# One transpose for the row maxima of a group of heads, and a new place for the expert matmuls between the attention steps

## The reference

```python
x = x + LN(attn(LN(x)))      # 16 heads of 16, rotary, causal, window of 250
x = x + LN(ffn(LN(x)))
# ffn: a second attention, 16 heads of 16, rotary, all 512 keys (no mask), rmsnorm, then
shared = swiglu(flat @ W_shared_in) @ W_shared_out
h = swiglu(flat @ W1_shared)
for e in range(8):
    routed = routed + h @ W2_experts[e] * w[:, e:e + 1]   # w: top 2 of 4 in the group chosen
out = rmsnorm(x + shared + routed)
```

## Time and profile before

| | us |
|---|---|
| runs of the kernel before | 2071.21, 2077.92, 2048.68 |
| median | 2071.21 |
| profiled execution, its own time | 2052.56 |
| its span, first to last instruction | 2050.8 |
| TensorE busy (PE) | 1887.0 (92%) |
| VectorE busy (DVE) | 1405.9 (69%) |
| ScalarE busy (ACT) | 829.9 (40%) |
| GpSimd busy (POOL) | 376.7 (18%) |
| granted TensorE clock, mean | 0.954 of full speed |

### The profile page before, as it was taken

The page is one execution under the profiler, slowest core; times in us unless marked ns, Lnnn a source line. Parts: engine busy times, 40 slices in busy tenths (PEclk is TensorE's granted clock), DMA queues, the critical chain, the costliest instruction groups (busy, mean ns, idle before and its releaser), DMA issues.

```text
span 2050.8 us, 28564 instructions
## 1 busy us (share of the span) xinstructions
PE 1887.0 (92%) x9436; PEld 1053.9 (51%) x9436; DVE 1405.9 (69%) x4368; ACT 829.9 (40%) x1730; POOL 376.7 (18%) x669
## 2 busy tenths in 40 slices
PE   6868899999999999999999999999999999999987
PEld 4343363745556364654637455563645546364456
DVE  6447475685778668684876857786676857768367
ACT  3432535335342644335353353426433353533410
POOL 1327014101231012200141012310122101420010
PEclk8565899999999999999999999999999999999999
DMA  3016002201022100311022010221003110130420
GB/s 106 2 62 246 22 22 84 83 2 52 22 94 83 43 11 23 134 43 42 32 89 88 2 52 22 94 83 43 11 23 134 43 43 32 47 119 2 175 82 11
DMA packets 28227, 123.09 MB, mean 60 GB/s; under 512 B 3888, under 2 KB 14768, under 8 KB 23472
## 3 DMA queue, kind: packets, MB, share of 16 engines
q1 hardware_dynamic: 25552, 105.54, 14.1%
q0 software_dynamic: 2528, 15.73, 2.0%
HBM read 101.33 MB, written 18.87 MB: 59 GB/s over the span
## 4 chain that ended last, share of the span: by engine, by line
PE 65%; DVE 26%; issue 6%; ACT 3%; DMA 1%; SPq 0%; POOL 0%; DVEq 0%; ACTq 0%; POOLq 0%
PE ot L780 11%; PE fb L841 10%; PE sm L738 8%; DVE negmax L1194 6%; PE fb L819 5%; PE st L766 5%; PE st L706 3%; PE fb L815 3%; DVE sm L1191 2%; PE st L722 2%; DVE acc L1392 2%; PE fb L837 2%; PE sm L766 2%; PE dn L706 2%; PE dn L792 2%
## 5 line engine op out<-in xcount | busy, mean ns | idle before, releaser
L618 ACT ACTIVATE probs<-st 128x512 f32<-128x512 f32 (+3 forms) x832 | 397.7, 506 | 422.5 <-PE st L766 417.4
L841 PE MATMUL fb<-w_r,h_r 128*128 128x512 f32 x1344 | 388.9, 418 | 0.0
L738 PE MATMUL sm<-k_t,q_t 48*128 48x512 f32 (+3 forms) x864 | 318.7, 449 | 58.3 <-DVE negmax L1191 28.9
L1194 DVE TENSOR_REDUCE negmax<-sm 128x1 f32<-128x512 f32 x416 | 269.4, 685 | 82.1 <-PE sm L738 82.0
L766 PE MATMUL st<-q_t,k_t 64*128 64x512 f32 (+3 forms) x832 | 301.8, 452 | 20.9 <-ACT probs L618 19.9
L738 PEld LDWEIGHTS sm<-k_t,q_t 48*128 48x128 f32 x864 | 144.4, 194 | 316.1 <-DVE negmax L1191 144.8
L841 PEld LDWEIGHTS fb<-w_r,h_r 128*128 128x128 f32 x1344 | 232.7, 189 | 93.2 <-issue 55.8
L1191 DVE CUSTOM_DVE_ANT_0 sm<-sm,mask_qk 128x384 f32<-128x384 f32 (+1 forms) x448 | 203.6, 468 | 112.0 <-PE sm L738 108.4
L780 PE MATMUL ot<-probs,v_s 128*32 128x512 f32 (+3 forms) x2048 | 259.6, 539 | 2.3 <-POOL probs L493 2.3
L452 POOL TENSOR_TENSOR stack<-rot,stack 128x256 fp32r<-128x256 f32 x64 | 50.0, 782 | 1017.4 <-ACT stack L554 1017.4
L766 PEld LDWEIGHTS st<-q_t,k_t 64*128 64x128 f32 x832 | 133.4, 192 | 118.5 <-ACT probs L618 79.2
(11 more groups left out here) (210 smaller groups left out, 2769.1 us busy)
## 6 DMA issues: line engine op xcount, KB each, us to landing
w_r<-w_parts SPq DMA_DIRECT2D x30, 2048.0 KB, 8.0
wup_r<-wup_parts SPq DMA_DIRECT2D x32, 512.0 KB, 4.2
w_parts<-w_r POOLq DMA_DIRECT2D x4, 2048.0 KB, 9.0
x_s<-in_L_attn_query SPq DMA_DIRECT2D x8, 512.0 KB, 4.9
q_t<-rot_b SPq DMA_DIRECT2D x256, 4.0 KB
x_kept<-o_s SPq DMA_DIRECT2D x8, 512.0 KB, 3.1
h_s<-in_L_ffn_W_experts POOLq DMA_DIRECT2D x8, 512.0 KB, 4.9
xa<-x_kept SPq DMA_DIRECT2D x8, 512.0 KB, 3.3
```

What stands on the lines that cost most here:

```text
L618: nc.scalar.activation(probs[:, n % PSLOTS, 0:hi - lo], score_bank(m)[:, 0:hi - lo], ACT.Exp, scale=float(D) ** -0.5).then_inc(s_ex, 1)
L738: mm(max_bank(w, a)[:, 0:hi - lo], q_t[r:r + MROW, b, t * P:(t + 1) * P], k_t[r:r + MROW, b, lo:hi], start=True, stop=True).then_inc(s_sm, 1)
L841: last = mm(fb[q % 2][:, :], h_r[:, h, m, rows], w2_r[:, k % 2, w, m, :], start=(m == 0 and n == 0), stop=(m == NH - 1 and n == 2))
L1194: return v.tensor_reduce(negmax[:, g % 2, n // GH, c:c + 1], max_bank(g * UNITS + n, a)[:, 0:hi - lo], AX.X, ALU.max, negate=True).then_in ...
```

## The change

There are two edits.

First, the four transposes of `max_rows` become one. The split maxima are laid out so that all 32 values of a row (2 halves of the array's rows, 2 parts, 2 heads, 4 tiles) stand side by side, and one transpose of 128x32 puts them into 32 partitions of `dn`, 128 columns wide. ScalarE copies 32x128 in place of 8x512. The four DMAs of a group carry the same bytes, each from 8 partitions of 512 bytes in place of 2 of 2048.

Second, expert pieces move. `QUIET` (first body) becomes 3, 7, 11 and so on to 59, and 61, where it was spread evenly over 6 to 60 (6, 9, 13, 16, 20, 24, 27, 31, 34, 38, 42, 45, 49, 52, 56, 60). `QUIET_OUT` (second body) goes from n = 2, 8, 12 (4, 8, 12 in the first group) to n = 6, 10, 14 (6, 10, 12 in the last). The pieces of the lead end one step earlier in the first body. The split of the hidden rows follows five steps behind its matmul, where it was three.

```diff
-QUIET = spread(4 * NH, 6, 60)
-QUIET_OUT = [g * UNITS + n for g in range(NGR) for n in ((2, 8, 12) if g else (4, 8, 12))]
-HIDDEN_AT = spread(8 * NH - len(QUIET), 4 - LEAD, 3) + QUIET
+QUIET = list(range(3, 60, GH)) + [61]
+QUIET_OUT = [g * UNITS + n for g in range(NGR) for n in (6, 10, 14 if g < NGR - 1 else 12)]
+HIDDEN_AT = spread(8 * NH - len(QUIET), 4 - LEAD, 2) + QUIET
...
-ACT_LAG, DVE_LAG, HIGH_LAG = 1, 2, 3
+ACT_LAG, DVE_LAG, HIGH_LAG = 1, 2, 5
...
-        m_split = sb("m_split", [P, 2, NT, 2, 2, 2], F32R)
-        m_t = rot_b[0:8].rearrange("p h d -> p (h d)")
+        m_split = sb("m_split", [P, 2, 2, 2, 2, NT], F32R)
+
+        M_ROWS = 8 * NT
+        m_t = rot_b[0:M_ROWS].rearrange("p h d -> p (h d)")[:, 0:P]
...
-                            r, m = SK * half + MROW + part, 4 * half + 2 * part
+                            r, m = SK * half + MROW + part, 2 * NT * (2 * half + part)
                             sp.dma_start(q_t[r:r + 1, 2 * g:2 * g + 2, :].bitcast(F32),
-                                         rot_b[m:m + 2].rearrange("p h d -> p (h d)")).then_inc(s_mr[g % 2], 16)
+                                         rot_b[m:m + 2 * NT].rearrange("p h d -> p (h d)")[:, 0:P]
+                                         ).then_inc(s_mr[g % 2], 16)
...
-                copy(m_t, dn[0:8, :]).then_inc(s_mc, 1)
+                copy(m_t, dn[0:M_ROWS, 0:P]).then_inc(s_mc, 1)
...
-                for t in range(NT):
-                    last = nc.tensor.transpose(
-                        dn[0:8, t * P:(t + 1) * P],
-                        m_split[:, g % 2, t].bitcast(F32).rearrange("p h j b -> p (h j b)"), ident[:, :])
+                last = nc.tensor.transpose(dn[0:M_ROWS, 0:P],
+                                           m_split[:, g % 2].bitcast(F32).rearrange("p h j b t -> p (h j b t)"),
+                                           ident[:, :])
                 last.then_inc(s_mp, 1)
...
-                m = negmax[:, g % 2].rearrange("p t (b h) -> p t h b", b=2)
-                hi = m_split[:, g % 2, :, :, 0, :]
-                lo = m_split[:, g % 2, :, :, 1, :]
+                m = negmax[:, g % 2].rearrange("p t (b h) -> p h b t", b=2)
+                hi = m_split[:, g % 2, :, 0]
+                lo = m_split[:, g % 2, :, 1]
```

## The result

| | us |
|---|---|
| runs of the changed kernel | 2124.18, 2167.89, 2115.39, 2127.41 |
| median of all four | 2125.8 |
| ratio to the kernel before | 1.0335, 95% interval 1.0287 to 1.0384 |
| profiled execution, its own time; span | 2124.18; 2122.4 |
| granted TensorE clock, mean (before) | 0.932 (0.954) |

The account below looks back on a forecast made before the run. TensorE was taken to bound both middles, VectorE the second body's lead. 7 x (2.6 - 0.9) = +11.9, entry 0 -3.6 and clock -6.2, together +2.1 on 2052.56, gave 2055 us, range 2018 to 2085.

Parts of the forecast that it names:

- The row of four: Four steps without an expert piece between them take about 2.35 us, two separate pairs 1.32: about 1.0 us lost.
- 2.6 us per entry: Second body: 2.1 us longer in the first group, 1.4 in the second, 0.85 gained in the third, tail 0.
- The tail has four banks, and I see no new wait: 0: Second body's tail: the moved expert pieces were to cost nothing there.
- The first body: First body as a whole: 0.9 us gained per entry, with 0.35 by step 39, 0.33 in the lead, 0.2 in the tail.
- fewer rows of four are new: two in the first group: First body: only steps 7 to 10 and 11 to 14 become new rows of four; step 12 is 1.2 us later.
- at step 19 only 0.3 are left: First body: of the 1.2 us delay at step 12, 0.3 remains at step 19, an expert piece being already done.
- The transposes and the subtraction: One transpose for four saves 0.33 us per call; VectorE's small subtraction no longer waits for GpSimd's, some 1.0 us per first body.
- The merges: Fewer changes between scores and expert work on TensorE: 0 to 0.1 us each, taken as 0, 8 us held for the range.
- the wait moves instead of going: Rival, chance 0.20: GpSimd's subtraction meets another small VectorE instruction near step 23, so that gain and the clock's fail: 2068 us.
- 2 x 3.1 = 6.2 us: Clock term: two falls to half clock in first bodies' middles (entries 6 and 7) go away, saving 6.2 us.
- bunching and the clock: Rival, chance 0.09: second bodies cost 4.5 us plus 3.1 for a clock fall each, first bodies gain nothing: +50, 2102 us.
- TensorE alone counts: Rival, chance 0.15: VectorE's slack swallows all bunching, leaving pure savings of 41 us: 2012 us.

Follow-up runs that it names:

- E1: The single transpose alone on the kernel before, with all expert pieces and lags as before; ratio 1.0057.
- E2: The moves and lags of the change alone on the kernel before, with its four transposes kept; ratio 1.044.
- E5: E1 with the split of the hidden rows five steps behind its matmul in place of three; ratio 0.9907 to the kernel before.
- E9: E5 with one expert piece of the second body moved from step 18 to 20; ratio 0.9993 to the kernel before.
- E7: The changed kernel with the scores of n = 4, 5, 8, 9, 12, 13 in second bodies' middles issued twice; ratio 1.0305 to the kernel before.
- E13: E5 with five maximum scores at the end of the second body's lead issued twice; ratio 0.9881 to the kernel before.
- E8: E1 with first bodies' score matmul of step 18 issued twice and that of step 21 three times; ratio 0.9922 to the kernel before.
- E10: E5 with the second body's expert pieces at n = 7, 11, 15 (7, 11, 12 in the last group); ratio 1.0414 to the kernel before.

## Why the prediction was wrong

**The row of four: right in kind and size.** 2.31 us measured for 2.35, waits of 0.54 for 0.54, a middle 2.1 us longer with one piece fewer. The term "2.6 us per entry" for the second body measured 2.1 + 1.2 = 3.3. What failed there is "The tail has four banks, and I see no new wait: 0": I had not counted that the tail takes over a piece. In it the transposes of the outputs then wait for ScalarE:

```profile
725.81 0.66 PE L795 MATMUL dn<-ident,o_t 128*128 128x128 f32 x4 [0.94 <-ACT o_t L558]
```

**The first body: wrong in sign, and the step that failed in the schedule.** Forecast -0.9, measured +0.8 - 0.3 + 1.5 = +2.0. The step that failed is "fewer rows of four are new: two in the first group", with "at step 19 only 0.3 are left". I priced the rows of four there by the second body's walk and let the owed work absorb them; in the trace six waits of 0.3 to 0.8 us stand from step 6 to step 35, not in the first group alone, since shorter scores bring TensorE sooner to the bank. Two bodies with different score widths needed two walks. The lead, forecast -0.33, was +0.8 by an edit that I had described but not priced.

**The transposes and the subtraction: right.** The forecast for them alone was 20 us, 49 calls at 0.33 and 3.6 in entry 0. E1 and E2 give 15 and 16, by the slope of 1.33, and entry 0 was 3.6 shorter, as forecast. The later split gained 10 us (forecast 7 x 1.0). The merges, put at 0, gave nothing that shows: from `weigh` to the expert work behind it is 1.00 us (684.42 to 685.42), as it was to the transposes. In the steady part of the changed kernel the small subtraction takes

```profile
L1209 DVE TENSOR_TENSOR m_split<-negmax,m_split x56: 178/180/331, 294.3 to 1972.0; 128x16 fp32r<-128x16 f32 x56
```

at most 0.33 us for the 1.20 of the earlier trace rows. The rival "the wait moves instead of going" is refuted: TensorE waits 0.55 us at step 22, as a row of four makes it, and not 1.04. GpSimd's subtraction near the end of the tail does meet other work now, VectorE's additions to `acc` (L1469, median 0.62 us, for 0.42 in the kernel before), but nothing waited for them. The rule of the Trainium skill ("SBUF — State Buffer", "Who interferes with whom") held: GpSimd's subtraction now lies over VectorE's statistics of `acc`, with one SBUF input (817.13, 0.42 us long beside GpSimd's 817.26), and they are not lengthened: their mean in the trace is 0.42.

The DMAs, put at 0 with 2 us as the dearest, were waited for a little more than in the earlier trace rows, and in entry 0 alone:

```profile
  PEld st L769: 2.5, 2
  PE st L769: 1.0, 2
```

**The clock: wrong in sign, and the largest miss of any term.** Forecast -6.2 us, measured +29 to +38. The step that failed is the term "2 x 3.1 = 6.2 us": it took two falls away and let the change's new waits cause none. They were left to the rival, at 0.09, for which I took "most entries had the same waits without a fall" as evidence of safety. It was evidence of nearness: in E1 three transposes fewer behind such a wait went with seven falls in seven entries where there had been two. One fall does not cost the 3.1 us of the earlier trace rows alone: in the second bodies where it came twice, middle and tail lost 3.6 and 5.3. In five second bodies of the changed kernel it came at a row of four, here in entry 4, step 22, and the `weigh` behind it:

```profile
1187.91 0.79 PE L742 MATMUL sm<-k_t,q_t 48*128 48x512 f32 x1 [0.50 <-DVE negmax L1197]
...
1188.64 1.94 PE L783 MATMUL ot<-probs,v_s 128*32 128x512 f32 x8
```

The same `weigh` took 1.07 at 684.42. The rival "bunching and the clock" was nearest with its +50, but not by its terms: the second body cost 3.3 and not 4.5, the first 2.0 and not 0, and the clock 4 to 5.5 us per entry and not 3.1. By the mean clock and the span, time at half clock went from 2 x 0.046 x 2050.8 = 189 us to 2 x 0.068 x 2122.4 = 289.

**"TensorE alone counts", 2012:** refuted for the changed kernel. Of its 41 us of savings E5 has 25, at equal clock.

What stays open: which of several like places falls in a given execution. E9's first bodies are E5's, instruction for instruction, and in four of seven the clock fell at steps 22 to 31, in E5's in none; E7 and E13 show falls that moved on when the waits before them were filled. No run here has the changed kernel's places with its clock held up.

## What to carry to other kernels

On an engine that is 92% busy, spreading the filler work evenly between units whose results another engine must drain is worth more than grouping it to save switches: with two banks a row of four steps costs 0.5 to 0.8 us of waiting each time. Price a move separately in each stage whose instructions have other sizes, count the pieces on both sides of every stage boundary, and price each constant of the diff. Before you predict a small gain on TensorE, look how near its idle stretches already are to a fall of the clock: what is saved as work is paid as idling, and at some 1.3 to 1.5 us per 0.001 of mean clock it can turn the sign; where an engine waits anyway, a repeated matmul can be worth having.

## What the runs showed of the hardware

Taking work from TensorE made the kernel slower (E1, 1.0057), and adding useless matmuls to it made it faster (E8, 0.9922; E13 at no cost in its lead). The clock fell behind waits of only 0.5 to 1.05 us each (E1 and the changed kernel), and in E5 within a 6.10 us stretch in which TensorE was busy for 5.52, while the same stretch of another entry kept it. In E10 it stayed at 1.2 GHz for 55.80 us in which TensorE was busy for 52.58.

Time at half clock costs less here than half of itself: 1.33 us per 0.001 of mean clock, over 2 x 0.001 x 2050 = 4.1 us of half-clock time, is a third. By the clock's record single falls cost somewhat more, 3.1 us for 6.8 at half clock in the earlier trace rows, 3.6 for 10.2 and 5.3 for 13.7 in entry 4 of the changed kernel. One reason shows in the rows: from start to start the same work takes less than twice as long (`weigh` 1.87 us, 1188.64 to 1190.51, for 1.00). That other engines set the pace in part of that time is likely, and no run shows it apart. The Trainium skill, "TensorE: Matmul & The Clock Gate", "HAM oscillation — how this bites in real kernels", reckons the loss as half of the throttled time; by that rule the extra 100 us would have cost 50, an estimate, and not 29 to 38.
